# Self-attention at the end of a two-layer kernel: 128-row second matmuls in the first unit, another way back for batch 0's output rows, and its feed-forward work placed later

## The reference, cut to what matters

```python
def _L1_ffn_ref(x, Wq, Wk, Wv, Wo, g1, b1, g2, b2, Wg, W1, W2):   # 16 heads of 8, 8 experts, top 2
    xn = layer_norm(x, g1, b1)
    q, k, v = heads(xn @ Wq), heads(xn @ Wk), heads(xn @ Wv)
    attn = jax.nn.softmax(jnp.einsum('bhqd,bhkd->bhqk', q, k) / np.sqrt(dk), axis=-1)
    o = merge(jnp.einsum('bhqk,bhkd->bhqd', attn, v)) @ Wo
    x = x + o
    xf = layer_norm(x, g2, b2).reshape(B * S, D)
    gate = xf @ Wg
    topv, topi = jax.lax.top_k(gate, TOP_K)
    probs = jax.nn.softmax(topv, axis=-1)
    cw = jnp.sum(jax.nn.one_hot(topi, N_EXPERTS) * probs[..., None], axis=1)
    h = jax.nn.relu(jnp.einsum('td,edh->teh', xf, W1))
    moe = jnp.einsum('ted,te->td', jnp.einsum('teh,ehd->ted', h, W2), cw).reshape(B, S, D)
    return x + moe
```

## Time and profile before

| what | value |
|---|---|
| median of 3 executions | 430.06 us (428.94 to 433.03) |
| the profiled execution, its own time | 426.66 us |
| its span | 424.6 us |
| PE busy | 378.9 us, 89% of the span |
| DVE busy | 268.0 us, 63% |
| ACT busy | 234.1 us, 55% |
| GpSimd busy | 69.7 us, 16% |
| mean granted TensorE clock | 0.963 of 2.4 GHz |

### The profile page before, as it was taken

The page is one execution under the profiler, slowest core; times in us unless marked ns, Lnnn a source line. Parts: engine busy times, 40 slices in busy tenths (PEclk is TensorE's granted clock), DMA queues, the critical chain, the costliest instruction groups (busy, mean ns, idle before and its releaser), DMA issues.

```text
span 424.6 us, 6424 instructions
## 1 busy us (share of the span) xinstructions
PE 378.9 (89%) x2311; PEld 199.3 (47%) x2311; DVE 268.0 (63%) x556; ACT 234.1 (55%) x681; POOL 69.7 (16%) x123
## 2 busy tenths in 40 slices
PE   3797998998989989999659989899989988989996
PEld 2355664695555633777345654521222232224444
DVE  3568886747872328545685774795678878652252
ACT  2267687845883376101675836144677776786320
POOL 5032380002000200002162020034010005020020
PEclk9898999999999999899898999985999999999999
DMA  8930000000000000000000005500254000000000
GB/s 203 253 86 1 2 0 2 0 2 2 1 2 2 1 0 0 2 0 2 1 2 0 2 0 180 119 2 0 74 154 73 2 1 2 1 2 0 26 1 25
DMA packets 15423, 13.02 MB, mean 31 GB/s; under 512 B 3521, under 2 KB 13984, under 8 KB 15392
## 3 DMA queue, kind: packets, MB, share of 16 engines
q1 hardware_dynamic: 14830, 11.72, 10.9%
q10 hardware_dynamic: 561, 0.90, 0.9%
HBM read 8.88 MB, written 3.67 MB: 30 GB/s over the span
## 4 chain that ended last, share of the span: by engine, by line
PE 67%; DVE 15%; ACT 10%; DMA 3%; issue 2%; POOL 2%; SPq 1%; ACTq 0%; DVEq 0%
PE pC L689 7%; PE pS L577 7%; PE pT L368 6%; PE pC L419 4%; PE pS L406 4%; PE pT L519 4%; ACT PT L890 4%; PE pC L451 4%; PE pT L752 3%; PE pS L681 3%; DVE nm L1124 3%; PE pT L438 2%; DVE mx L1369 2%; PE pT L313 2%; PE pC L381 2%; PE pC L458 2%
## 5 line engine op out<-in xcount | busy, mean ns | idle before, releaser
L1369 DVE TENSOR_REDUCE mx<-pS 128x2 f32<-128x1024 f32 x64 | 76.3, 1220 | 26.0 <-PE pS L681 25.6
L890 ACT ACTIVATE PT<-pS,nm 128x154 f32<-128x154 f32 x136 | 51.7, 422 | 10.5 <-DVE nm L1124 10.5
L1004 ACT ACTIVATE PT<-pT 128x512 f32<-128x512 f32 x83 | 47.5, 607 | 16.4 <-PE pT L752 13.3
L1124 DVE TENSOR_REDUCE nm<-pS 128x4 f32<-128x616 f32 x48 | 37.6, 794 | 11.0 <-PE pS L406 10.9
L689 PE MATMUL pC<-PT,space 128*32 128x512 f32 x256 | 36.6, 646 | 2.1 <-ACT PT L1004 1.9
L406 PE MATMUL pS<-space 64*128 64x154 f32 x384 | 34.1, 300 | 4.9 <-ACT PT L890 3.4
L1469 POOL TENSOR_SCALAR ve<-mv 128x4 f32<-128x4 f32 x10 | 2.3, 230 | 199.5 <-DVE mv L1062 199.5
L681 PE MATMUL pS<-space 48*128 48x512 bf16 x128 | 30.6, 404 | 3.3 <-DVE space L1384 1.7
L406 PEld LDWEIGHTS pS<-space 64*128 64x128 f32 x384 | 28.1, 188 | 9.6 <-ACT PT L890 3.5
L752 PE MATMUL pT<-space 50*128 50x512 bf16 (+1 forms) x83 | 31.1, 401 | 1.6 <-DVE space L1112 0.5
L1004 ACT ACTIVATE PT<-pC 128x512 f32<-128x512 f32 x45 | 27.4, 608 | 6.3 <-PE pC L752 4.5
(11 more groups left out here) (248 smaller groups left out, 666.2 us busy)
## 6 DMA issues: line engine op xcount, KB each, us to landing
space<-parts_scratch SPq DMA_DIRECT2D x8, 288.0 KB, 6.0
parts_scratch<-space SPq DMA_DIRECT2D x4, 384.0 KB, 2.7
parts_scratch<-space SPq DMA_DIRECT2D x4, 256.0 KB, 3.1
space<-parts_scratch SPq DMA_DIRECT2D x8, 96.0 KB, 2.4
x<-in_x_dram SPq DMA_DIRECT2D x2, 256.0 KB, 4.4
space<-in_L_xattn_Wq_dram SPq DMA_DIRECT2D x1, 512.0 KB, 4.8
space<-in_L_xattn_Wo_dram SPq DMA_DIRECT2D x1, 512.0 KB, 7.2
space<-in_L_ffn_up_w_dram SPq DMA_DIRECT2D x1, 512.0 KB, 7.3
```

Source lines behind the costliest of these rows:

```text
L890: last = A.activation(pq(n, u, q).rearrange("p (i k e) -> p i k e", i=2, e=2)[:, j // 2, :, j % 2], ps[:, c:c + T], ACT.Exp, bias=nm[:, u ...
L1004: A.activation(PT[:, 4 * kt + j, :], ps[:, :], ACT.Exp, scale=SSCALE)\
L1124: V.tensor_reduce(nm[:, u % 2, q, :], ps[:, :].rearrange("p (e k) -> p e k", e=2)[:, :, 0:2 * T].rearrange("p e (i k) -> p i e k", i=2), A ...
L1369: V.tensor_reduce(mx[:, u % 2, k // 2, j:j + 2], ps[:, :].rearrange("p (i k) -> p i k", i=2), AX.X, ALU.max).then_inc(freed(("ss", u, k)), 1)
```

## The change

The first unit's second matmuls take selm and mT over all 128 partitions instead of 8. GpSimd clears Wk of layer 1 and a 128-partition selm beforehand, so that the added rows are zero. Batch 0's `row_project` goes to ring W; ACT copies it to a new tile back0, GpSimd adds that to y, and DVE only takes the statistics, one key tile later. In `ffn1_first`, xt moves from kt = 0 to kt = 2 of the sixth unit, the gate from kt = 1 to kt = 3, the ups to kt = 2 and 3 of the seventh, weight_rows and weights to kt = 1, 2 and 3 of the eighth. `combine` goes from GpSimd to DVE. The downs leave the eighth unit for the tail, where they stand among fewer `warm` matmuls.

```diff
@@ tiles
-        mT = xa[1].Wk[0:2 * G4, :].bitcast(BF16).rearrange("p (i s) -> p i s", i=2)
+        mT = xa[1].Wk[:, :].bitcast(BF16).rearrange("p (i s) -> p i s", i=2)
+        back0 = m.take(QT * D)
-        selm = sb("selm", [2 * G4, G4, P], BF16)
+        selm = sb("selm", [P, G4, P], BF16)
@@ tensor
             def ffn1_first(u, kt):
                 u -= len(units[2]) - 3
-                if (u, kt) == (0, 0):
+                if (u, kt) == (0, 2):
                     xt(4, 0, "W")
-                if (u, kt) == (0, 1):
+                if (u, kt) == (0, 3):
                     gate(1, 0, "S")
-                if (u, kt) == (0, 2):
+                if (u, kt) == (1, 2):
                     up(1, 0, 0)
-                if (u, kt) == (0, 3):
+                if (u, kt) == (1, 3):
                     up(1, 0, 1)
-                if (u, kt) == (1, 2):
+                if (u, kt) == (2, 1):
                     weight_rows(1, 0, "W")
-                if (u, kt) == (1, 3):
+                if (u, kt) == (2, 2):
                     weights(1, 0, 0)
-                if (u, kt) == (2, 0):
+                if (u, kt) == (2, 3):
                     weights(1, 0, 1)
-                if u == 2:
-                    downs(1, 0, kt, (0, 1))
...
-                    ps = claim("S", ("sproj", b))
+                    ps = claim("S" if b else "W", ("sproj", b))
...
                     values(u, QT - 1, pv)
+                downs(1, 0, 0)
                 back(len(uu) - 1)
-                warm("W", 4)
+                downs(1, 0, 1)
                 row_outT(B - 1)
                 warm("W", 4)
                 row_project(B - 1)
-                warm("C", 20)
+                for e in (2, 3):
+                    downs(1, 0, e)
+                warm("C", 11)
@@ scalar
                     if u >= 2:
                         act.wait_ge(mrow_ready, 16 * 4 * (u - 1))
-                    cp(mT[:, u % 2, :], ps[0:8, 0:256].bitcast(BF16)).then_inc(freed(("smT", u)), 1)
+                    if u == 0:
+                        act.wait_ge(selm_ready, 1)
+                    cp(mT[0:2 * G4, u % 2, :], ps[0:2 * G4, 0:256].bitcast(BF16)).then_inc(freed(("smT", u)), 1)
...
+                def row_back():
+                    ps = filled(act, ("sproj", 0))
+                    cp(back0, ps[:, :]).then_inc(freed(("sproj", 0)), 1)
...
                         if u and g == 0 and kt == 1:
                             row_outT(b - 1)
+                        if u and g == 0 and kt == 2:
+                            row_back()
@@ vector
             def ffn1_first(u, kt, half):
                 u -= len(units[2]) - 3
-                if u == 0 and 3 <= 2 * kt + half <= 6:
-                    ranks(0, (2 * kt + half - 3,))
                 if (u, kt, half) == (0, 3, 1):
+                    logits1(0)
+                if (u, kt, half) == (1, 2, 0):
+                    ranks(0)
                     chosen(0)
-                if (u, kt, half) == (1, 0, 0):
+                if (u, kt, half) == (1, 3, 1):
                     shares(0)
-                if (u, kt, half) == (1, 3, 1):
+                    combine(0)
+                if (u, kt, half) == (2, 2, 0):
                     weights(1, 0, 0)
-                if (u, kt, half) == (2, 0, 1):
+                if (u, kt, half) == (2, 3, 0):
                     weights(1, 0, 1)
-                if (u, kt, half) == (2, 3, 1):
-                    downs(1, 0)
...
+                def row_statistics():
+                    dve.wait_ge(y_ready, 1)
+                    statistics(4, 0)
...
-                        if u and g == 0 and kt == 2:
-                            row_project(b - 1)
+                        if u and g == 0 and kt == 3:
+                            row_statistics()
                         ffn1_first(u, kt, 1)
                 back(len(uu) - 1)
                 row_project(B - 1)
+                downs(1, 0)
                 normalise(4, B - 1)
@@ gpsimd
+            for c in range(H1 // 2):
+                taken(pool, ("kT", 1, c))
+            seq(G.memset(xa[1].Wk[:, :], 0.0))
             seq(G.memset(selm[:, :, :], 0.0))
...
             for u in range(2, per + 2):
                 parts(u)
+            taken(pool, ("sproj", 0))
+            row = y[:, 0, :, :].rearrange("p q d -> p (q d)")
+            G.tensor_tensor(row, back0, row, ALU.add).then_inc(y_ready, 1)
             norm(4, 0)
             normalise()
+            parts(per + 2)
             add_rows(0)
-            for u in range(per + 2, B * per):
-                parts(u)
-                if u == per + 2:
-                    combine()
+            parts(per + 3)
             norm(4, 1)
             add_rows(1)
```

More of the change, by code:

```diff
@@ L257, in build @@
         mrow_ready = sem("mrow_ready")
+        y_ready = sem("y_ready")
         selm_ready = sem("selm_ready")
@@ L758, in self_attention @@
                                 score_pair()
-                                if u == len(uu) - 1:
-                                    ffn1_first(u, kt)
                             if j == 2 and kt == 0 and u:
@@ L781, in self_attention @@
                             self_values(1, "W")
[L782 to L785, removed]
+                        ffn1_first(u, kt)
                     values(u, QT - 1, pv)
+                downs(1, 0, 0)
                 back(len(uu) - 1)
-                warm("W", 4)
+                downs(1, 0, 1)
                 row_outT(B - 1)
@@ L1252, in gate, with logits1, ranks @@
                 tt(p3, r, p2, ALU.subtract).then_inc(cparts_ready, 1)
[L1254 to L1261, removed]
+            def logits1(b):
+                ps = filled(dve, ("gate", 1, b))
+                V.tensor_copy(lg[:, b, :, :].rearrange("p q e -> p (q e)"), ps[:, 0:QT * E])\
+                    .then_inc(freed(("gate", 1, b)), 1)
+            def ranks(b):
+                taken(dve, ("gate", 1, b))
+                for q in range(QT):
                     seq(V.max(top[:, b, q, :], lg[:, b, q, :]))
                     seq(V.max_index(topi[:, b, q, :], top[:, b, q, :], lg[:, b, q, :]))
-                if qs[-1] == QT - 1:
-                    tt(ex[:, b, :, 0], top[:, b, :, 1], top[:, b, :, 0], ALU.subtract).then_inc(lg_ready, 1)
+                tt(ex[:, b, :, 0], top[:, b, :, 1], top[:, b, :, 0], ALU.subtract).then_inc(lg_ready, 1)
             def shares(b):
@@ L1333, in ffn1_first @@
                 u -= len(units[2]) - 3
-                if u == 0 and 3 <= 2 * kt + half <= 6:
-                    ranks(0, (2 * kt + half - 3,))
                 if (u, kt, half) == (0, 3, 1):
+                    logits1(0)
+                if (u, kt, half) == (1, 2, 0):
+                    ranks(0)
                     chosen(0)
-                if (u, kt, half) == (1, 0, 0):
+                if (u, kt, half) == (1, 3, 1):
                     shares(0)
-                if (u, kt, half) == (1, 3, 1):
+                    combine(0)
+                if (u, kt, half) == (2, 2, 0):
                     weights(1, 0, 0)
-                if (u, kt, half) == (2, 0, 1):
+                if (u, kt, half) == (2, 3, 0):
                     weights(1, 0, 1)
-                if (u, kt, half) == (2, 3, 1):
-                    downs(1, 0)
             def ffn1_last():
-                ranks(1, range(QT))
+                logits1(1)
+                ranks(1)
                 chosen(1)
@@ L1580, in add_rows @@
                 G.tensor_tensor(x[:, b, :, :], x[:, b, :, :], y[:, b, :, :], ALU.add).then_inc(xb_ready, 1)
[L1582 to L1594, removed]
             per = len(units[2]) // B
```

## The result

The changed kernel takes 414.81 us in the median of 4 executions (413.46 to 415.74), beside 429.5 us (426.45 to 433.03) for the kernel before. The ratio is 0.9683, 95% interval 0.9634 to 0.9731: 3.2% faster. The forecast was 419.2 us in a range from 415.5 to 424.5. The measured median lies 0.7 us under that range; the ratio, put on 430.06 us, gives 416.4.

A forecast was written before the change was run, and what follows sets the result against it. PE, over 90% busy in nearly all self-attention, taking turns with ACT, plus a first-unit clock fall; -4.6 - 1.9 - 3.8 + 2.1 - 2.8 + 0.1 = -10.9 us, from 430.06 to 419.2 us, range 415.5 to 424.5.

The forecast's parts named there:

- Part 1: First unit: second matmuls on 128 rows keep the clock up, 15.8 us against 20.44, -4.6 us.
- Rival A: First unit: rows are not what keeps the clock, the fall at 284.4 stays; 423.8 us, chance 0.12.
- Part 2: Fifth unit: batch 0's row leaves by ACT and GpSimd, so no pair waits for DVE's addition; -1.9 us.
- Parts 3 to 5: Sixth unit loses the ups, -3.8 us; seventh gains them, +2.1; eighth loses the downs but gains weight_rows and weights, -2.8.
- Rival D: Units six to eight: moved pieces find other waits and half is given back; 422.5 us, chance 0.15.
- Part 6: Tail: downs replace a wait for ACT's copy and 13 warm matmuls; +0.1 us.
- B: Eighth unit: the clock falls for a short time, costing 3 to 4 us; 423 us, chance 0.10.
- C: Clock falls in the eighth unit and stays down through the tail; slower than before, 436.8 us, chance 0.03.

The follow-up runs named there:

- experiments 1: Kernel before with only selm and mT widened to 128 partitions and their clearing on GpSimd; 423.36 us, ratio 0.9812.
- 6: Kernel before with 128 rows and batch 0's row by ACT and GpSimd, feed-forward pieces at their old places; 430.97 us, ratio 1.0067.
- 7: Kernel before with 128 rows and only the downs, with DVE's addition to x, moved to the tail; 423.19 us, spread too wide for a ratio.
- 2: Changed kernel with selm and mT on 8 partitions again and no clearing; 418.87 us, ratio 0.9754 against the kernel before.
- 3: Kernel before with selm and mT over 32 partitions; 427.59 us in one execution.
- 4: Kernel before, unchanged, profiled once more; 426.07 us.
- 8: Changed kernel with batch 1's transposes one key tile later, in the second unit, its products later too; 417.74 us, ratio 0.9757 against the kernel before.
- experiment 5: Changed kernel with batch 0's row again through ring S and DVE's addition at kt = 2; 416.47 us, ratio 0.9666 against the kernel before.

## Why the prediction was right

*The reading of before.* Beside the four units that it calls longer, the second lasts 15.98 us (300.29 to 316.27), where batch 1's queries, keys and values are made; the change leaves it alone, so the sum did not suffer. The other fall that it names began at 171.7 us, not 171.9, and PE had been idle for 0.38 us at 169.6, so it was a fall with little idle time, not with none.

*Part 1, size 4.6, measured 3.96.* The mechanism holds: 8 and 32 rows fall, 128 rows do not. The step of 0.32 us and the wait for GpSimd (1.2 predicted, 1.22 measured) were right. Missed was a wait of 0.89 us for DVE: in the first unit it reduces ten pairs, not eight, and adds the projection before them; a wait for a reduction that I did not count once PE was fast again. It is the main part of the 0.7 us by which the unit's 16.48 us pass 15.8: 11.36 + 2.56 for the second matmuls + 0.59 for the transposes + 1.22 + 0.89 are 16.62. The rule of the Trainium skill (TensorE: Matmul & The Clock Gate, "Why this matters for your kernels"), that drops in mid-kernel come of idle gaps, fits experiments 1, 6 and 7 in kind: there the falls came just behind 1.70 us of idle PE (1 and 7) and 2.2 us into a stall (6), though these gaps are shorter than the one that the Trainium skill warns of. It does not explain 2, 3 and 4, where PE was busy throughout, nor the fall in the eighth unit of 8. Rival A falls.

*Part 2, 1.9, measured 1.78.* Shown by experiment 5. The step that it needs, room for GpSimd's rows, was forecast at 5.7 us into the sixth unit and came at 5.7.

*Parts 3 to 5, -3.8, +2.1, -2.8; measured -3.89, +1.82, -2.89.* Reading the extra of each unit against the third, between the same values, gave every size within 0.3 us. Experiment 7 shows the downs' share by itself: 3.35 us less, of which weight_rows and the first weights, moving in, take back 0.46. Neither xt nor weight_rows waits for GpSimd or DVE in the changed kernel's profile. Rival D falls.

*Part 6, +0.1, measured +0.19.*

*Sum, 10.9, measured 10.5 in the parts that the change touches.* The 10.5 owe a little to luck: part 1 was put 0.64 us too high as a gain, the seventh unit 0.28 too high as a loss. The medians differ by 14.7 us, which the sum did not have, and so the measured 414.81 lies under the range while the ratio falls inside it. In the profiles, 2.4 us of the difference lie ahead of the self-attention, which no part of the change explains. The rest is likely how often other falls strike; only the profiled executions show where. The lowest executions, 424.58 of the 42 of before that ran beside the experiments and 413.42 of 10 after, differ by 11.2 us, close to the sum; the medians of the same, 430.5 and 415.5, by 15.0. Experiments 1 and 7 show one such fall, behind the fifth unit's stall, which part 2 removes along with the stall; it cost 2.3 and 4.9 us in units five and six. No profile of the kernel before itself caught one there, so its share in the 4 us by which the medians' difference passes the sum stays open.

*Rivals B and C.* B was given 0.10 and 3 to 4 us. The fall does occur, costs 7.1 us (experiment 8) and reaches into the tail as C had it, yet not through it: it healed at 393.8 us, before the gate and ups. So the price of B was put at half, and in the changed kernel itself no profile caught that fall.

## What to carry to other kernels

Pick one plain repetition of a loop as the measure, and read every special one against it between the same instructions: the difference is the price of the extra work, with all hiding already in it. A stall of PE costs its own length; in two of six profiles with the 1.70 us stall a fall of the clock came behind it and cost 2.3 and 4.9 us more. Judge a removal of filler work by both. Move a producer to a slower path only together with its consumer: without it, the medians had lost all that part 1 had gained, by a stall of 3.70 us and the fall of the clock that came with it.

## What the runs showed of the hardware

- With PE busy without a gap, the granted clock fell when the second matmuls of a 48-row stream had 8 or 32 rows (in four of four profiles, for 13.7 us each), and stayed when they had 128 (in ten of ten), though the added rows were zeros and the steps the same 0.32 us.
- The same code had its short falls, of 3.4 us each, at different moments in two profiles of the kernel before: 14.7, 38.6, 171.7, 205.9 and 222.9 us in one, 37.4, 174.0 and 221.7 in the other.
- A PE idle for 1.70 us in the fifth unit brought a fall in two profiles (6.8 and 13.7 us long) and none in four others. A fall of 17.1 us that began in the eighth unit, with no idle time of PE over 0.26 us ahead of it there, cost 7.1 us; the same instructions had none in the changed kernel's two profiles.
- A fall did not end because PE was busy: in the kernel before PE was busy 13.13 of the 13.6 us (284.4 to 298.0) that it was at the lower level.
